# Attention on one core: stores of the split q and k issued from ScalarE's queue instead of SyncE's

## The reference, cut to what matters

```python
# block 0: 16 heads of 8 channels, one shared k and v, rotary embedding, causal
q = (x @ Wq + bq).reshape(Bx, Tx, HEADS, HD)
k = (x @ Wk + bk)[:, :, None, :]
...
att = jnp.einsum('bthd,bThd->bhtT', q, k) / math.sqrt(HD)
att = jnp.where(causal, -jnp.inf, att)
att = jax.nn.softmax(att, axis=-1)
out = jnp.einsum('bhtT,bThd->bthd', att, v).reshape(Bx, Tx, Cx)
return out @ Wo + bo
# block 1: 16 heads of 8 channels, q and k normalised over all channels, not causal
q = l2norm(q)
k = l2norm(k)
...
attn = jnp.einsum('bhnd,bhkd->bhnk', q, k)
attn = attn / temperature
attn = jax.nn.softmax(attn, axis=-1)
out = jnp.einsum('bhnk,bhkd->bhnd', attn, v)
```

## Time and profile before

| | us |
|---|---|
| median of 3 runs (lowest, highest) | 2208.63 (2202.42, 2208.76) |
| the profiled execution | 2208.01 |
| its span, first to last instruction | 2206.3 |
| PE busy in the span | 1799.6 (82%) |
| DVE busy | 1409.2 (64%) |
| ACT busy | 1162.2 (53%) |
| POOL busy | 928.2 (42%) |
| mean granted TensorE clock | 0.882 |

### The profile page before, as it was taken

The page is one execution under the profiler, slowest core; times in us unless marked ns, Lnnn a source line. Parts: engine busy times, 40 slices in busy tenths (PEclk is TensorE's granted clock), DMA queues, the critical chain, the costliest instruction groups (busy, mean ns, idle before and its releaser), DMA issues. The chain is left out here.

```text
span 2206.3 us, 41497 instructions
## 1 busy us (share of the span) xinstructions
PE 1799.6 (82%) x13060; PEld 939.0 (43%) x13060; DVE 1409.2 (64%) x2467; ACT 1162.2 (53%) x2814; POOL 928.2 (42%) x1035
## 2 busy tenths in 40 slices
PE   4798888887167357999999996389999999999996
PEld 2344444435156223333333222245555555555552
DVE  5566667654211345776777782468888788888872
ACT  0265555560033014766666673067777677776771
POOL 3255455441411421122222111267667677666760
PEclk9599999896589557998999997699999999999996
DMA  2122222223133311222222222311111111111210
GB/s 70 50 83 87 79 82 86 78 75 102 52 93 87 112 54 51 87 86 77 76 87 90 86 75 78 115 33 30 44 37 34 37 38 50 41 39 41 53 42 17
DMA packets 98742, 145.42 MB, mean 66 GB/s; under 512 B 13528, under 2 KB 51611, under 8 KB 98456
## 3 DMA queue, kind: packets, MB, share of 16 engines
q1 hardware_dynamic: 96536, 139.33, 20.2%
q0 software_dynamic: 2048, 4.16, 0.7%
HBM read 78.74 MB, written 49.28 MB: 58 GB/s over the span
## 5 line engine op out<-in xcount | busy, mean ns | idle before, releaser
L1230 DVE TENSOR_REDUCE M_sb<-banks 128x1 f32<-128x512 f32 (+3 forms) x1024 | 549.0, 581 | 293.3 <-PE banks L831 147.8
L1026 ACT ACTIVATE probs_sb<-banks 128x512 f32<-128x512 f32 (+3 forms) x1024 | 473.4, 516 | 324.5 <-PE banks L866 319.2
L831 PE MATMUL banks<-K_sb,Q_sb 72*128 72x512 bf16 (+3 forms) x1024 | 375.7, 372 | 48.4 <-issue 20.8
L866 PE MATMUL banks<-Q_sb,K_sb 75*128 75x512 bf16 (+3 forms) x1024 | 359.8, 358 | 37.4 <-DMA Q_sb<-mrows_sb 31.2
L882 PE MATMUL banks<-probs_sb,V_sb 128*32 128x512 f32 (+3 forms) x2048 | 250.2, 555 | 6.4 <-POOL probs_sb L1119 5.2
L831 PEld LDWEIGHTS banks<-K_sb,Q_sb 72*128 72x128 bf16 x1024 | 105.1, 103 | 316.1 <-DVE M_sb L1230 164.8
L2201 ACT ACTIVATE l_p_sb<-banks,l_nb_sb,l_inv_sb 128x128 f32<-128x128 f32 x512 | 228.1, 465 | 10.7 <-DVE l_nb_sb L2373 9.9
L2287 POOL TENSOR_TENSOR l_pn_sb<-l_p_sb,l_rs_sb 128x512 f32<-128x512 f32 x128 | 150.1, 1172 | 144.2 <-DVE l_rs_sb L2379 142.7
L2279 POOL TENSOR_TENSOR l_inv_sb<-l_clip_sb,l_minus_half_sb 128x16 f32<-128x16 f32 x64 | 186.2, 2910 | 56.0 <-DVE l_clip_sb L2348 54.1
L2272 POOL TENSOR_TENSOR l_ts_sb<-l_t_sb 128x1024 f32<-128x1024 f32 x64 | 153.2, 2394 | 42.4 <-DVE l_t_sb L2327 25.6
L866 PEld LDWEIGHTS banks<-Q_sb,K_sb 75*128 75x128 bf16 x1024 | 102.9, 101 | 136.3 <-ACT probs_sb L1026 32.3
(11 more groups left out here) (258 smaller groups left out, 3426.1 us busy)
## 6 DMA issues: line engine op xcount, KB each, us to landing
Q_sb<-qk_dram SPq DMA_DIRECT2D x192, 96.0 KB
o_dram<-osum_sb SPq DMA_DIRECT2D x64, 256.0 KB, 2.6
l_vs_sb<-l_vt_sb SPq DMA_DIRECT2D x112, 128.0 KB, 2.3
qk_dram<-parts_sb SPq DMA_DIRECT2D x96, 128.0 KB
K_sb<-qk_dram SPq DMA_DIRECT2D x32, 288.0 KB
spack_sb<-o_dram SPq DMA_DIRECT2D x16, 256.0 KB, 3.6
opack_sb<-o_dram SPq DMA_DIRECT2D x16, 256.0 KB, 3.7
x<-xnew_sb SPq DMA_DIRECT2D x16, 256.0 KB, 5.5
```

What stands on the lines that cost most here:

```text
L831: mm = pe.matmul(out[:, 0:width], g.Q[0:RK, par, q, h, k * P:(k + 1) * P], g.K[0:RK, par, qk(q), hk(h), 0:width], start=True, stop=not causal)
L866: pe.matmul(SB[ring % 3][:, t0:N], g.K[0:RM, slot, qk(q), hk(h), k * P:(k + 1) * P], g.Q[0:RM, slot, q, h, t0:N], start=True, stop=True).t ...
L1026: act.activation(g.probs[:, k, h, t0:N], SB[ring % 3][:, t0:N], ACT.Exp, scale=scale)\
L1230: dve.reduce_max(g.M[:, u % 2, k, h:h + 1], SA[ring % 3][:, 0:width], AX.X, negate=True)\
```

## The change

ACT takes the six stores over from SP. It has a new step `store_made(i, w)`, which waits on `part3` and issues the three stores of one tensor on ACT's own DMA queue. In the first layer ACT does it after tiles 4 and 8 of the last quarter, in the second layer after tiles 2 and 5. SP drops the two calls there. `store_parts` stays on SP for the first two batches of a layer, which are prepared before the loop.

```diff
--- before.py
+++ after.py
@@ -782,9 +782,6 @@
                         if not first:
                             store(i)
                         sp.dma_start(g.xres[:, :], x[i - lo]).then_inc(s["x_loaded"], 16)
-                        if ahead:
-                            for w in range(2):
-                                store_parts(i + FIRST, w)
 
             def load_x(i):
                 sp.dma_start(g.xn[:, 0, :], x[i + (FIRST - lo)]).then_inc(f["x_loaded"], 16)
@@ -1071,6 +1068,15 @@
                 for w, at in enumerate(((1, 15), (2, 14)) if causal else ((2, 11), (2, 14))):
                     if (q, n) == at:
                         part2(i, w)
+                for w, at in enumerate(((3, 4), (3, 8)) if causal else ((3, 2), (3, 5))):
+                    if (q, n) == at:
+                        store_made(i, w)
+
+            def store_made(i, w):
+                act.wait_ge(ps["part3"], ahead_of(i, 2, w + 3))
+                for part in range(PARTS):
+                    act.dma_start(g.qk_dram[i + FIRST, w, :, part].rearrange("u d h n -> u (d h) n"),
+                                  g.parts[:, w, part, :]).then_inc(ps["parts_stored"], 16)
 
             def batch(i, slot, first, last, ahead, more):
                 for q in range(UNITS):
```

## The result

The changed kernel is slower: 2259.21 us as the median of four runs (2250.67 to 2266.22) against 2208.18 us before, a ratio of 1.0231 (95% interval 1.0201 to 1.0261), 51 us. The prediction, 2187 us and faster, was wrong in its sign, and the time lies outside its range.

The account below looks back on a forecast made before the run. PE was taken to bound attention, waiting on row-maxima moves late behind SP's stores. From 2208.0 us, -47 + 20 (ACT's issues) + 4 (lateness, clock) = -23, shaded to -21, gave 2187 us; range 2167 to 2222 us.

Parts of the forecast that it names:

- What bounds the kernel: In attention PE leads; its largest waits, 22.3 us, are on the move of row maxima, late behind SP's six stores.
- Gain: 47 us: Both attention layers: removing SP's store bursts takes away 22.3 us of PE's waits and 25 us of low clock behind them.
- the low clock behind them, 51.0 x 0.5 = 25 us: Seven stretches after PE's waits: 51.0 us at 1.2 GHz, each costing about 0.5 us, all to come back.
- the rival that the clock does not come back: Attention: clock drops fall elsewhere, only 2 us is won, 2206 us; chance 0.10.
- I take 0.66: ACT's last quarter: each store issue costs 0.66 us, 3.95 us for six, as on SP into an empty queue.
- the upper bound: Six stores issued behind other traffic in the second layer take 9.59 us; with the first layer's 6.13, ACT's cost reaches 67 us.
- The first rival, ACT pays what SP paid: ACT's issues behind traffic take 1.0 to 1.6 us each, stopping exponentials; 67 us against 47, 2228 us; chance 0.20.
- 6 x 1.9 = 11.4 us of the sum: Second layer, six batches: ACT's issuing beyond its idle time, 3.95 - 2.0 = 1.9 us each, falls on PE.
- ACT's own delay widens both, so I take 4 us: Batch-end move meeting the stores: room of 2.61 and 4.19 us widens, so lateness and clock lost to ACT's stalls cost 4 us.
- its rival, at 21 us: Next batch's start: the batch-end move lands late behind ACT's stores and PE waits, 21 us instead of 4; 2204 us; chance 0.12.
- 6 x 1.4 = 8.4 us in the sum: First layer, six batches: ACT's issuing beyond its usable idle time costs PE 1.4 us each, between 0.95 and 1.7.
- That POOL's third part costs no wait: The waits on `part3` moved to ACT cost nothing, since POOL makes the parts early enough before the stores.

Follow-up runs that it names:

- the last two runs: Against the kernel before, ACT issues the stores in the second layer only, bursts after tiles 0 and 6, then 2 and 3: 2221.54 us, 1.0038; 2230.98 us, 1.0077.

## Why the prediction was wrong

**What bounds the kernel** was read rightly. The late move behind SP's six stores is real: with smaller stores's waits vanish, and the time falls.

**"Gain: 47 us"** was too large by a quarter; the quarter-size stores on SP give 35 us (30 to 40 by the interval's ends on 2210 us). The waits of 22.3 us went. The term that failed is "the low clock behind them, 51.0 x 0.5 = 25 us". In that run's profile the drops that the first six lines of the earlier trace rows list are gone, but low clock stands elsewhere, also where PE waited at most 0.6 us at a time. Two windows of it (columns as in the earlier trace rows), one where a drop had been and one where a drop is now:

```profile
969.71:986.45 16.74, 16.05 (x90) 6.35 (x90) 13.55 (x22) 11.74 (x23) 0.89 (x4) 1.00 0.27 86
...
346.90:360.61 13.71, 12.83 (x88) 5.85 (x85) 7.63 (x18) 7.60 (x20) 6.00 (x14) 0.77 0.29 95
```

Over both layers, from move to move, the low clock fell from 99 to 82 us only: 17 of the 51.0 us came back, worth 9 us and not 25. This profile is of the slowest of the run's four executions (2182.88 us). In the profile of the quarter-size stores on ACT the low clock was 65 us, 34 us less than before, so how much comes back is known only as a third to two thirds, and the rival that the clock does not come back was as far true.

**"I take 0.66"** for every store on ACT was right for an issue that nothing holds (median 0.572 us, shortest 0.547) and wrong for the second burst of the second layer. The reason given, DMA engines busy for 0.33 of the time in the earlier trace rows, does not tell a free issue from a held one. Two windows of the change (columns as in the earlier trace rows), one from a free burst of the first layer up to the next burst, one over a held burst of the second layer, have the same DMA share of 0.40:

```profile
308.74:312.46 3.72, 3.15 (x26) 1.30 (x24) 2.04 (x6) 1.86 (x6) 2.57 (x7) 1.00 0.40 105
...
994.67:999.82 5.15, 2.89 (x18) 0.88 (x18) 2.65 (x5) 1.44 (x3) 0.00 (x0) 0.97 0.40 133
```

The nearest rows for an issue behind such stores were the 9.59 us of the earlier trace rows, which stood as the upper bound. The first rival, ACT pays what SP paid, is what happened in that layer, at a mean of 1.07 us a store: 19.4 us more of PE's waits on ACT than before, against the 6 x 1.9 = 11.4 us of the sum, and low clock behind them that the sum had nearly left out. The second layer's profile is 33.6 us longer than with quarter-size stores on SP (470.3 against 436.7).

**"ACT's own delay widens both, so I take 4 us"** is the step that failed in the first layer. The prediction saw that the stores would meet the batch-end move, had the 6.8 us landing of the earlier trace rows for it and the room of 2.61 us, and then counted on ACT's delay to make room. The move needed 5.75 to 6.6 us. And its rival, at 21 us, priced only the wait: the waits on the move were smaller, 8.8 us, but low clock followed four of the five, 40 us more of it in the six stretches, and these grew by 27.8 us. ACT's own part there, 6 x 1.4 = 8.4 us in the sum, was near: PE's waits on the exponentials and the mask behind them came to 7.9 us. What the sum had next to nothing for is the low clock behind both kinds of wait. How the 27.8 us divide between them is not shown by the change itself; the single stores, with the late move alone, made the same stretches 12.7 us longer. This rival held, and its price of 21 us lies between the two. The quarter-size stores take both away, and the stores of SP ahead of the move show the late move without ACT.

**The rivals were not alternatives.** The first came true in the second layer, the second in the first, so their prices came together, and the range, built on one at a time, ended at 2222 us.

That POOL's third part costs no wait was not tried by itself: PE's wait on POOL's mask in the first layer (9.9 us where the same query shows 5.2 before) grew by 4.7 us. By the order of POOL's program that is the mask behind a late exponential and not `part3`, which is argued and not shown. Nothing speaks against this step.

On the held issue the trace shows one thing that bears on a rule. SP's `keep` was issued in 0.35 us at 995.78, inside ACT's issue that began at 994.67 and took 1.67 us, and before it SP had issued nothing since the load of K at 989.05. The Trainium skill, Perfetto Trace Analysis, section DMA Instruction - HWDGE (DVE, Sync), lets a DMA instruction's time contain a wait for the lock on the shared descriptor generator; in this instance SP cannot have been the one that held ACT. Where SP's three loads were issued beside ACT's held burst, in the run with the stores after the move, the rows do not exclude it.

From issue to use, the late move took 5.75 to 6.6 us (change), 3.5 to 6.0 us (single stores) and 7.5 to 8.8 us (all on SP). The Trainium skill, DMA: Bandwidth & Descriptors, section Queues, rings and completion order, says that a DMA's semaphore is written only after every earlier write of that DMA engine, across its queues; by that a small move behind stores is late whichever engine issued them. These numbers agree with it. They would also come from plain sharing of the engines' time, and no run here separates the two.

**Left open**: whether the move is late by order or by shared time, and what an issue on ACT waits for (its own stores not yet drained, SP's loads, or both); the last two runs did not settle it, though the first layer's free bursts speak against its own stores alone.

## What to carry to other kernels

Before a DMA is moved to a compute engine's queue, list what small transfers with a short deadline fall behind its bytes in the new place, and price each with the longest landing that the trace shows behind such bytes, plus the low clock that follows a wait. The second queue frees only the issuer; a burst on a compute engine also stops its arithmetic when issues are held, so put on it few stores, one at a time, and leave on the old queue no more than the small transfers behind them have time for. A low mean share of the DMA engines does not say that an issue will be free. Rivals that sit in different stages are added, not weighed against each other.

## What the runs showed of the hardware

- An issue of a 128 KB store on ACT takes 0.55 to 0.6 us, and 0.32 us with 32 of the 128 rows, when nothing holds it; held, three of them took up to 6.8 us (stores after the move). ACT's arithmetic stands meanwhile (3.83 us before the exponential at 999.93). The DMA engines were busy for 0.40 of the time over a held burst, and for as much in the 3.7 us from a free one on.
- A 12 KB move needed 2.61 us from issue to use with no stores ahead of it. With stores of 128 KB issued in the few us before it or beside it, it needed 3.5 to 6.0 us (single stores on the other queue), 5.75 to 6.6 us (six of them there) and 7.5 to 8.8 us (six on its own queue).
- TensorE's granted clock fell to 1.2 GHz after most waits of 1 to 4 us, not after all, but two stretches without any wait above 0.6 us also had a mean of 0.77 and 0.82. With the waits removed, a third to two thirds of the low clock expected back came back; the rest stood elsewhere.
